# A four-layer sequence kernel: the time-neighbour stencil moves from TensorE to two HBM loads, and the first stage is put in another order

## What is computed

```python
def reference(x, ...):
    x = x + L0(x)   # masked softmax pooling over time
    x = x + L1(x)   # a diffusion stencil over channel and time
    x = x + L2(x)   # adapter (512 -> 128 -> 512) and layer norm
    x = x + L3(x)   # gated traces (running sums over time), three 512x512 matmuls, layer norm
    return x

def L1(y):          # y is x1, the result of the first layer
    yp_x = pad(y, channel, 1, mode='reflect')
    lap_x = yp_x[:, :, :-2] - 2.0 * y + yp_x[:, :, 2:]
    yp_y = pad(y, time, 1, mode='reflect')
    lap_y = yp_y[:, :-2, :] - 2.0 * y + yp_y[:, 2:, :]
    return zX * lap_x + zY * lap_y + zR * y * (1.0 - y)
```

## Time and profile before

| | us |
|---|---|
| median of 3 runs | 754.73 |
| lowest, highest | 752.50, 756.64 |
| span of the profiled execution | 750.7 |
| `front(0)` starts on PE | 191.15 |
| one turn of the main loop | 69.62 |
| PE busy | 701.7 (93%) |
| DVE busy | 552.5 (74%) |
| ACT busy | 336.6 (45%) |
| POOL busy | 128.8 (17%) |

### The profile page before, as it was taken

The page is one execution under the profiler, slowest core; times in us unless marked ns, Lnnn a source line. Parts: engine busy times, 40 slices in busy tenths (PEclk is TensorE's granted clock), DMA queues, the critical chain, the costliest instruction groups (busy, mean ns, idle before and its releaser), DMA issues.

```text
span 750.7 us, 8200 instructions
## 1 busy us (share of the span) xinstructions
PE 701.7 (93%) x2904; PEld 507.3 (68%) x2904; DVE 552.5 (74%) x779; ACT 336.6 (45%) x706; POOL 128.8 (17%) x203
## 2 busy tenths in 40 slices
PE   4989886886899999999999999999999999999986
PEld 1545343433586878687778868786877787787874
DVE  3645997399898659766975887597669758874964
ACT  2143432234435734472465347435723562465144
POOL 5002024053202200220031012102100220031001
PEclk9989999898999999999999999999999999999999
DMA  7885115441733332033305132412333051313001
GB/s 216 278 319 203 53 45 169 76 151 57 187 122 56 57 112 51 7 57 113 56 1 116 53 57 43 126 30 28 56 113 57 0 111 59 56 21 93 1 1 56
DMA packets 41095, 64.94 MB, mean 87 GB/s; under 512 B 8088, under 2 KB 10136, under 8 KB 41054
## 3 DMA queue, kind: packets, MB, share of 16 engines
q1 hardware_dynamic: 29118, 47.62, 18.3%
q0 software_dynamic: 8448, 16.78, 14.2%
q10 hardware_dynamic: 3488, 0.01, 0.3%
HBM read 48.54 MB, written 15.74 MB: 86 GB/s over the span
## 4 chain that ended last, share of the span: by engine, by line
PE 78%; DVE 9%; SPq 4%; issue 4%; ACT 3%; DMA 2%; POOLq 0%; DVEq 0%; POOL 0%; ACTq 0%
PE bank L1019 19%; PE bank L1021 19%; PE bank L1020 19%; PE bank L1059 4%; PE bank L1073 4%; PE bank L915 2%; PE bank L1002 2%; PE bank L1120 2%; PE bank L1080 2%; PE bank L1049 2%; PE bank L1013 2%; SPq L347 2%; DVE sqb L1398 1%; DMA x_scratch<-sqb 1%; DVE sqb L1407 1%
## 5 line engine op out<-in xcount | busy, mean ns | idle before, releaser
L1019 PE MATMUL bank<-xh,wg_l 128*128 128x512 f32 x256 | 104.0, 406 | 0.1
L1021 PE MATMUL bank<-xh,wg_h 128*128 128x512 f32 x256 | 100.3, 392 | 0.0
L1020 PE MATMUL bank<-xl,wg_h 128*128 128x512 f32 x256 | 99.9, 390 | 0.0
L552 POOL DMA_DIRECT2D xr<-rows_scratch x16 | 21.2, 1323 | 243.2 <-PE bank L1049 184.9
L1501 DVE TENSOR_TENSOR_SCAN tr<-alpha,carry,tr 128x512 f32<-128x512 f32 x48 | 58.9, 1269 | 0.0
L1019 PEld LDWEIGHTS bank<-xh,wg_l 128*128 128x128 f32 x256 | 48.2, 188 | 12.2 <-issue 2.4
L1020 PEld LDWEIGHTS bank<-xl,wg_h 128*128 128x128 f32 x256 | 48.1, 188 | 12.0 <-issue 1.9
L1021 PEld LDWEIGHTS bank<-xh,wg_h 128*128 128x128 f32 x256 | 48.1, 188 | 10.9
L1019 PE MATMUL bank<-th,wt_l 128*128 128x512 f32 x128 | 53.1, 415 | 2.0 <-DVE tl L1513 2.0
L1019 PE MATMUL bank<-xh,ws_l 128*128 128x512 f32 x128 | 53.5, 418 | 0.0
L544 POOL TENSOR_TENSOR xr<-xb 128x2040 f32<-128x2040 f32 x8 | 28.8, 3600 | 138.7 <-DVE sqb L1407 57.4
(11 more groups left out here) (214 smaller groups left out, 1564.1 us busy)
## 6 DMA issues: line engine op xcount, KB each, us to landing
xr<-rows_scratch POOLq DMA_DIRECT2D x16, 1024.0 KB, 9.6
xb<-in_x SPq DMA_DIRECT2D x8, 1024.0 KB, 14.0
x_scratch<-sqb SPq DMA_DIRECT2D x7, 1024.0 KB, 4.5
xr<-x_scratch SPq DMA_DIRECT2D x7, 1024.0 KB, 5.5
result<-xr SPq DMA_DIRECT2D x7, 1024.0 KB, 4.3
xb<-in_xT SPq DMA_DIRECT2D x3, 1024.0 KB, 9.5
xt<-in_xT SPq DMA_DIRECT2D x2, 1024.0 KB, 6.7
sqb<-in_xT SPq DMA_DIRECT2D x2, 1024.0 KB, 10.5
```

Of the source, the lines that this page charges most:

```text
L552: po.dma_start(xr[:, q % 2], rows_dram[b:b + 1, i].rearrange("(p c) e -> p c e", p=1) .broadcast_to([P, GT, E]), accum_op=ALU.add).then_in ...
L1019: pe.matmul(acc, wl, xh_, start=start, stop=False)
L1020: pe.matmul(acc, wh, xl_, start=False, stop=False)
L1021: return pe.matmul(acc, wh, xh_, start=False, stop=stop)
```

## The change

1. **Time neighbours.** x1 is stored in HBM (`x1_scratch`, T + 2 rows per batch; rows 0 and T+1 are the reflected ones). For each group SP loads the rows shifted by -1 into `nb` (`load_before`), and POOL adds the rows shifted by +1 by an accumulating DMA (`add_after`). `time_part`, `edges`, `edge_high`, `edge_low`, `squares` and `mix` are gone, and so are the store and load of x2.
2. **x2 by group.** For group q: ACT makes `wide = MID - zR * x1` (`mix_local`, 2048 elements), POOL multiplies it by x1 (`local`, 2048) and makes the channel neighbours in `xr` (`channels`, 2040), DVE adds `zY * nb` (`times`, 2048) and `zX * ...` (`stencil`, 2048). Groups 0 and 1 are made in the first stage; groups 2 to 7 are made in turns g = 1 to 6 of the loop. x1 of groups 1 to 7 comes back from HBM into `x1s` (`load_x1`).
3. **Operand pairs.** `xh, xl` and `th, tl` swap their roles from turn to turn (`x3_pair`, `trace_pair`, `product_pair`); `ph, pl` are gone. The freed SBUF holds stages for the weights, which are loaded without waiting for a buffer; their low parts are made by POOL.
4. **First stage.** `hidden(1, 0)` and `hidden(1, 1)` come after the first pooled tiles, the adapter of group 0 stands between the last tiles of batch 0, and `pooled` of batch 1 turns over four banks.

```diff
-                    def edges(b, j):
...
-                    def store_x2(b, j):
...
+                    def store_x1(b, j):
+                        sp.wait_ge(x1_done, NT * b + GT * (j + 1))
+                        sp.dma_start(rows_of_x1(b, j, 0), xb[:, b, part(j)]).then_inc(done, 16)
...
+                    def load_before(q):
+                        x1_landed(sp, b, j - 1)
+                        x1_landed(sp, b, j)
+                        if q:
+                            sp.wait_ge(x2_done, q)
+                        sp.dma_start(nb[:], rows_of_x1(b, j, -1)).then_inc(nb_in, 16)
+                    def load_x1(q):
+                        x1_landed(sp, b, j)
...
+                            sp.wait_ge(mix_v, q)
+                            sp.wait_ge(chan, 3 * q)
+                        sp.dma_start(x1s[:], rows_of_x1(b, j, 0)).then_inc(x1s_in, 16)
...
                     for g in range(GROUPS - 1):
+                        if g and g + 2 < GROUPS:
+                            load_x1(g + 2)
+                            load_before(g + 2)
                         sp.wait_ge(o_done, GT * g + GT)
...
-                        if g + 2 < GROUPS:
-                            sp.wait_ge(o_out, 16 * (g + 1))
-                            load_group(sp, g + 2)
...
+                    def local(q):
+                        po.wait_ge(mix_u, q + 1)
+                        po.tensor_tensor(flat(wide[:]), flat(wide[:]), flat(x1_of(q)), ALU.mult).then_inc(mix_v, 1)
+                    def channels(q):
...
+                            po.wait_ge(x1s_in, 16 * q)
...
+                        elif q > 1:
+                            po.wait_ge(o_out, 16 * (q - 1))
+                        po.tensor_tensor(s[:, :, 1:E - 1], xg[:, :, 0:E - 2], xg[:, :, 2:E], ALU.add)\
+                    def add_after(q):
+                        po.wait_ge(nb_in, 16 * (q + 1))
+                        x1_landed(po, b, j)
+                        x1_landed(po, b, j + 1)
+                        po.dma_start(nb[:], rows_of_x1(b, j, 1), accum_op=ALU.add).then_inc(nb_sum, 16)
...
+                        if g and g < LAST:
+                            local(g + 1)
+                            channels(g + 1)
+                            if g + 2 < GROUPS:
+                                add_after(g + 2)
...
+                        if g and adapted:
+                            mix_local(g + 1)
                         n1_gelu(g)
...
-                    def time_part(b, c):
...
+                    def times(q):
+                        ve.wait_ge(nb_sum, 16 * (q + 1))
+                        ve.wait_ge(mix_v, q + 1)
+                        ve.scalar_tensor_tensor(flat(nb[:]), flat(nb[:]), coef[:, ZY, b:b + 1], flat(wide[:]),
+                                                ALU.mult, ALU.add).then_inc(mix_t, 1)
...
+                        if mixing:
+                            times(g + 1)
                         logits(g, 0)
                         traces(g, 0)
                         logits(g, 1)
+                        if mixing:
+                            stencil(g + 1)
```

More of the change, by code:

```diff
@@ L1182, in _ @@
                     weight_sums(0)
-                    hidden(1, 0)
                     replicate(0)
@@ L1632, in _ @@
-                    stencil(1, 2)
-                    mix(1, 12)
-                    mix(1, 13)
+                    x1(1, 2)
+                    x1(1, 3)
+                    for c in range(GT):
+                        ln_apply(0, c)
+                    for c in range(4, 8):
+                        x1(1, c)
+                    times(1)
+                    x1(1, 8)
+                    x1(1, 9)
+                    stencil(1)
+                    x1(1, 10)
+                    x1(1, 11)
```

657 lines of the change are left out of this document (262 added, 395 removed).

## The result

| | before | after |
|---|---|---|
| median of 6 runs, us | 754.50 | 772.55 |
| lowest, highest | 751.88, 756.64 | 771.37, 777.66 |
| span of the profiled execution | 750.7 | 775.8 (its time: 777.66) |
| first MOD product of the loop | 202.38 | 182.23 |
| turn 0, then turns 1 to 6 | 69.8, 69.6 each | 70.0, then 76.5 to 77.8 |

The change makes the kernel slower: ratio 1.0249, 95% interval 1.0225 to 1.0274. The prediction was 737.5, with 717 to 755 as its range, and 0.77 for faster. It was wrong. (In the experiments one execution of the kernel before took 812.6 us at a granted clock of 0.845; it is left out of the ratios.)

What follows compares the result with a forecast made beforehand. TensorE bounds the loop (69.62 us a turn) but waits in the first stage. Span 750.7 - 31.1 (first stage) + 1 (turn 0) + 13 (turns 1 to 6) = 733.6; with the median 4.0 above, 737.5 us, range 717 to 755.

Steps and rivals of the forecast that it cites:

- Turns 1 to 6: Loop: `times` and `stencil` delay VectorE, so TensorE waits 2.1 to 2.2 us before `soma_in(g, 0)` each turn, 13 us in all.
- first rival: Loop: GpSimd runs `channels` before VectorE's `times`; TensorE waits 4.9 us a turn, 753.5 us in all; chance 0.13.
- `times` ahead of L547: Loop sign: VectorE's `times` starts right after GpSimd's `local` and before its `channels` (L547).
- POOL first, and the clock falls: Loop: `channels` before `times`, 4.9 us waits, and TensorE's clock falls, 2.9 us more each turn: 771 us; chance 0.07.
- the case without the clock: Loop: GpSimd's `channels` goes before `times`, TensorE waits 4.9 us a turn at unchanged clock: 753.5 us; chance 0.13.
- The forecast's own number: Whole kernel: 737.5 us, from a span of 733.6; chance 0.52 for 724 to 746.
- Steps (a) to (c): First stage: first pooled tile at 47.4, `x1(0, 7)` ends at 63.5, neighbour sum through HBM lands at 93.
- (d): First stage, from neighbour sum to `front(0)`: `stencil(0)` ends at 100.5, batch 1's first tile at 126.2, `front(0)` at 160.
- one wait of about 12 us before 95: First-stage sign: TensorE idles about 12 us before 95, released by VectorE's score read.
- The lock: VectorE and GpSimd share an SBUF port; whichever starts first holds it for its whole instruction, so start order decides.

Runs made afterwards that it cites:

- Experiment 3: The changed kernel with the mixing arithmetic of groups 2 to 7 cut to a few elements, waits and DMAs kept: 732.88 us in one run.
- experiment 8: The changed kernel with a different operation and inputs for GpSimd's `local` in each of groups 2 to 7: 4.62 us from two tiles, 3.6 from one.
- experiment 4: The kernel before with 4 to 10 extra 512-element VectorE steps ahead of `logits(g, 2)` in turns 1 to 6: 775.57 us.
- experiment 9: The changed kernel with GpSimd's `local` multiplying x1 by itself in groups 2 to 7, all else kept: 737.95 us, ratio 0.9776.
- Experiment 7: The changed kernel with batch 1's softmax steps and tanh moved ahead of first-stage waits on VectorE and ScalarE: 776.43 us, ratio 1.0312.

## Why the prediction was wrong

**What bounds the kernel, the place of the new wait, the releaser:** right. The waits stand before `soma_in(g, 0)` in turns 1 to 6, released by the addition of `logits(g, 2)`; nothing else in the loop is late. Experiment 3 confirms the rest: without the mix the turns are 69.62.

**The step that failed** is in "Turns 1 to 6": "POOL's `local` 3.6". That size came from a row of `channels`' kind, which reads one tile at two offsets; `local` reads two tiles and takes 4.63 (experiment 8). With 4.63 in the prediction's own sum `local` ends at 342.1, behind the 341.58 at which the store has landed, so its own first rival decides. The page GPSIMD Engine Reference of the Trainium skill, section "3.1 Elementwise — side-by-side cycle accounting", has 4497 ns for an addition of two float32 inputs of this length; the traces agree for two tiles (4.49 to 4.63 us) and not for one tile read twice (3.6), of which it says nothing. I took the nearer row, and it was the wrong kind. The same 3.6 stood for the low part of wo, which reads two tiles as well and took 4.52. What followed is the opposite of the sign that I gave (`times` ahead of L547), and turns of over 75 us, which I had named as a sign of being wrong.

**The rival** "POOL first, and the clock falls", with 0.07, is what happened: wait 4.9 predicted, 5.2 measured; 2.9 for the clock, 2.4 measured; 771 against 772.55. That the total is so close is in part luck: by this rival's terms the span is 766.6 and the loop starts at 172.3, and the profiled execution has 775.8 and 182.23. It had its point of decision, a margin of 0.5 us, and "the same order of events in each of the turns" was held against it. That argument was empty: the same margin in each turn makes the outcome the same in each turn, whichever it is. A margin of 0.5 us in a sum with a borrowed duration should have had nearly even odds. Nor were the wait and the clock two cases: every turn with a wait near 5 us, here and in experiment 4, cost 1.6 to 3.0 us beyond it. The other bound was wrong as well: the prediction let the clock fall only from somewhere above 2.6 us of wait, and in experiment 4 it was lower behind one of 2.04. The range's upper end, 755, held the case without the clock (753.5) and left out the one with it.

**The forecast's own number** was met by experiment 9 at 737.95, but not by its own terms. Its loop starts late: the first MOD product is at 179.0, where 172.3 was forecast. Its waits are 1.3 us and cost 1.5 a turn, where 2.2 was forecast. That is +6.7 and -4 on the span (736.4, forecast 733.6), and the median lies 1.6 us above it where I put 4.0. The errors cancel; the mechanism is confirmed by the turns, not by the total. The 4.0 was a wrong size too: in every run that lists both, a time is 1.7 to 2.1 us above its own span. The rest of the 4.0 is that the execution profiled before was a fast one.

**First stage.** Steps (a) to (c), and (d) as far as `stencil(0)`, hold within 1.2 us: the first pooled tile starts at 48.4 (47.4), `x1(0, 7)` ends at 64.1 (63.5), the x1 stores are issued at 66.6 and 67.4 (66.1, 66.9), the neighbour sum is there at 91.8 (93), `stencil(0)` ends at 101.2 (100.5). The 12.3 us between 160 and 172.3 come in (d). TensorE starts the first tile of batch 1 at 131.2, forecast 126.2. (In that stretch the forecast's own terms, 100.5 + 3.1 + 3.8 + 2.2 + 3.5, give 113.1 and not 112.5.) The roots end at 145.9, forecast 136.5: 3.6 of it is ScalarE's wait for the wn1 load, which the sum had at nothing:

```profile
139.35 0.63 ACT L798 ACTIVATE wn_h<-wn_l_f 128x512 fp32r<-128x512 f32 x1 [3.64 <-DMA wn_l_f<-in_wn]
```

Six of the nine executions with this first stage do not have this wait (in experiment 9 `front(0)` starts at 168.9, and TensorE's wait before the x3 transposes is 7.4 us in place of 11.0). Against those six the forecast of 160 is 6.4 to 9.2 us early. Why the load is late in the others is not shown. GpSimd held VectorE three times, not once, for 4.2, 0.7 and 2.9 us; a fourth time, 2.0 us on `stencil(0)`, eats what the neighbour sum had won. Two of them, on `ln_apply` and `stencil(1)`:

```profile
146.04 4.91 DVE L1427 SCALAR_TENSOR_TENSOR xr<-tr,rs_a,xr 128x512 f32<-128x512 f32 x1 [0.51 <-POOL rs_a L586]
...
160.47 5.22 DVE L1375 SCALAR_TENSOR_TENSOR xr<-xr,coef,nb 128x2048 f32<-128x2048 f32 x1
```

The forecast sign "one wait of about 12 us before 95" came, at 13.15 us, but with another releaser: ScalarE's tanh, behind the copy of the gate weights that waits for its load. Experiment 7 took it away and gained nothing.

**The lock.** That VectorE and GpSimd keep each other out, and that the order of starting decides, was right, and was what made the sum so sharp. Experiment 9 shows the other order: `channels` 5.34 us, since `times` had started 0.46 us ahead of it. SBUF — State Buffer, section "SBUF: two separate sides", of the Trainium skill says that whichever starts first has the pair for the whole instruction; 5.59 in one order and 5.34 in the other agree.

## What to carry to other kernels

Take a GpSimd step's duration from a row with the same operands, not only with the same length: whether its inputs are one tile or two changed it by a quarter. Where two engines that lock each other out start within a microsecond of one another, treat the order as open, price both, and force it by a semaphore if one is cheap: here one wait gave back 22 us. And before moving work away from a step that TensorE waits for, look whether that step itself can stand sooner in its own engine's queue; with the order forced, 1.9 us of it ahead of 5.9 us of other work took the whole cost of the six turns away. And before a difference between two profiles is called the effect of an edit, compare executions of which the edit did not touch that stage: here they differ by 6 us.

## What the runs showed of the hardware

- GpSimd, two float32 inputs, 2040 or 2048 elements a partition: 4.5 to 4.6 us from two tiles, 3.6 us when both inputs are one tile, for additions and multiplications alike.
- A VectorE step of 2.35 us with two SBUF inputs took 5.59 when GpSimd had started 0.14 us earlier; a GpSimd step of 3.59 took 5.34 when VectorE was 0.46 us ahead.
- TensorE's clock after a wait: waits of 2.6 us in one kernel cost 2.9 us (clock 1.00 behind it) or 4.5 (0.61), with the same instructions ahead of them. In experiment 4 one of 2.04 brought a lower clock (0.63) and one of 2.77 did not (1.00); a wait of 2.4 brought 0.83 in one execution and 1.00 in another of the same instructions. The waits of 4.8 to 5.2 us in the changed kernel and the one of 4.95 in experiment 4 brought the lower level, for 1.6 to 3.0 us on top.
